# One core: pairs of edge tiles with one addition a pair in the first attention layer, and part of its weighing on VectorE

## What is computed

```python
score = jnp.einsum('ehc,ehc->eh', q[dst], k[src]) / np.sqrt(C)   # H = 4 heads of C = 64
m = jax.ops.segment_max(score, dst, num_segments=N)
ex = jnp.exp(score - m[dst])
denom = jax.ops.segment_sum(ex, dst, num_segments=N)
alpha = ex / denom[dst]
msg = alpha[:, :, None] * v[src]
agg = jax.ops.segment_sum(msg, dst, num_segments=N)
out = agg.reshape(N, H * C) + h @ Wskip + bskip
return x + jax.nn.relu(out)
```

## Time and profile before

| | |
|---|---|
| median of 3 runs | 8399.73 us (8396.39 to 8405.45) |
| the profiled execution, its own time | 8395.49 us |
| its span | 8393.8 us |
| busy over the whole span: PE, DVE, ACT, POOL | 70%, 63%, 37%, 62% |
| first layer's loop, start of its first and its last score product | 681.8 and 1947.0 us |
| DVE, PE, ACT, POOL busy in 900 to 1100 us | 172.94, 159.41, 169.91, 134.34 of 200.00 us |
| granted TensorE clock, DMA share there | 0.96, 0.61 |

### The profile page before, as it was taken

One profiled execution on the slowest core, in us unless ns is written; L12 is line 12 of the kernel. 1 busy time (PEld: TensorE's weight loads), 2 busy tenths in 40 slices (PEclk: granted clock), 3 DMA queues, 4 the chain that ended last, 5 costly groups with the idle time before them and its releaser, 6 DMA issues. The chain is left out here.

```text
span 8393.8 us, 114926 instructions
## 1 busy us (share of the span) xinstructions
PE 5911.5 (70%) x29083; PEld 4485.9 (53%) x29083; DVE 5252.3 (63%) x14320; ACT 3102.5 (37%) x9138; POOL 5186.5 (62%) x5153
## 2 busy tenths in 40 slices
PE   6586777774399555556688888965577775574398
PEld 5234555553387234444577777754455553453387
DVE  9867888887665576665544444446677777435544
ACT  1245888887422300000333333312344444312322
POOL 0475666665577677777677777756777771433422
PEclk9798999996599877778699999967789986686599
DMA  5475666563366333333111111116333343473366
GB/s 147 152 247 160 171 173 172 170 172 115 108 207 200 111 102 101 100 102 103 28 28 32 31 28 32 26 27 193 102 105 103 105 100 117 150 229 95 100 204 199
DMA packets 633946, 1017.21 MB, mean 121 GB/s; under 512 B 136434, under 2 KB 436482, under 8 KB 631948
## 3 DMA queue, kind: packets, MB, share of 16 engines
q0 software_dynamic: 241920, 540.19, 24.2%
q1 hardware_dynamic: 391436, 470.18, 17.7%
HBM read 790.98 MB, written 222.86 MB: 121 GB/s over the span
## 5 line engine op out<-in xcount | busy, mean ns | idle before, releaser
L4099 POOL DMA_INDIRECT gat_edges_rows<-gat_table,gat_room x1080 | 1115.5, 1033 | 340.9 <-issue 322.4
L2825 POOL DMA_INDIRECT l_edges_ring<-pairs,first_room x832 | 843.8, 1014 | 472.5 <-issue 242.2
L2387 POOL DMA_INDIRECT l_sum_rows<-l_feats,back_room x832 | 827.0, 994 | 265.7 <-issue 241.9
L2407 PE MATMUL l_sum_o<-l_sum_rows,l_sum_s 128*128 128x256 f32 x1664 | 604.4, 523 | 468.3 <-DVE l_sum_s L2418 220.4
L2876 ACT ACTIVATE l_edges_ring<-l_edges_ring,l_edges_weight 128x64 f32<-128x64 f32 x3328 | 816.4, 335 | 0.0
L2407 PEld LDWEIGHTS l_sum_o<-l_sum_rows,l_sum_s 128*128 128x128 f32 x1664 | 410.9, 261 | 655.0 <-DVE l_sum_s L2418 325.5
L2948 PE MATMUL l_edges_o<-l_edges_ring,l_edges_sf 128*128 128x260 f32 x1664 | 534.9, 427 | 149.8 <-DVE l_acc L3081 141.1
L3717 ACT ACTIVATE m_ffn_ht<-m_ffn_hp,m_ffn_b1t 128x256 f32<-128x256 f32 (+1 forms) x598 | 270.7, 453 | 815.5 <-PE m_ffn_hp L3684 810.3
L2429 DVE TENSOR_TENSOR l_acc<-l_acc,l_sum_o 128x256 f32 x832 | 350.1, 421 | 351.3 <-PE l_sum_o L2407 258.4
L3694 PE MATMUL m_ffn_yp<-m_ffn_w2b,m_ffn_ht 128*128 128x256 f32 x2156 | 502.1, 385 | 30.4 <-ACT m_ffn_ht L3717 29.8
L3684 PE MATMUL m_ffn_hp<-m_ffn_xt,m_ffn_w1b 128*128 128x256 f32 (+1 forms) x2392 | 509.0, 366 | 11.5 <-DVE m_ffn_xt L3733 7.2
(11 more groups left out here) (899 smaller groups left out, 14604.4 us busy)
## 6 DMA issues: line engine op xcount, KB each, us to landing
sorted_rows<-l_proj_zero SPq DMA_DIRECT2D x44, 1032.0 KB
m_ffn_w1b<-in_L_ffn_w SPq DMA_DIRECT2D x32, 1024.0 KB, 6.4
m_ffn_w2b<-in_L_ffn_w SPq DMA_DIRECT2D x32, 1024.0 KB, 5.4
m_ffn_xs<-sorted_rows SPq DMA_DIRECT2D x120, 258.0 KB, 3.6
m_ffn_w1b<-in_L_ffn_W SPq DMA_DIRECT2D x57, 512.0 KB, 4.6
m_ffn_w2b<-in_L_ffn_W SPq DMA_DIRECT2D x57, 512.0 KB
m_by_node<-gat_edges_ys SPq DMA_DIRECT2D x96, 256.0 KB
l_proj_taken<-m_by_node SPq DMA_DIRECT2D x28, 768.0 KB, 6.9
```

The costliest lines, as they stand in the source:

```text
L2387: pool.indirect_dma_start(rows[:, slot, j, :], None, table, bass.IndirectOffsetOnAxis(ap=L.src[:, t:t + 1], axis=0)).then_inc(got[slot], 16)
L2407: pe.matmul(o[:, j, 0:D], s4[:, q % S4, j, :], rows[:, slot, j, :], start=True, stop=True).then_inc(out_done, 1)
L2825: pool.indirect_dma_start(rows(q, 0, 2 * D)[:, j, :], None, table, bass.IndirectOffsetOnAxis(ap=L.src[:, t:t + 1], axis=0)).then_inc(got[q ...
L4099: pool.indirect_dma_start(rows[:, slot, j, :], None, table, bass.IndirectOffsetOnAxis(ap=L.src[:, q * B + j:q * B + j + 1], axis=0)).then_ ...
```

## The change

The list is now cut into pairs of columns (`group=2`): both tiles of a pair belong to one block. That gives 391 pairs and 49 more visits of pairs, 440 pairs or 880 tiles, 220 quads, 55 chunks (`SortedList.tiles`). The two matmuls of a pair add up in one PSUM bank (`start` on the first, `stop` on the second), and VectorE adds once a pair. In odd quads ScalarE weighs three tiles (12 multiplications) and VectorE the fourth in one instruction (`weigh_last`), in step q+10 right behind `onehot`; a semaphore, `eighth`, tells PE and ACT. The ring of selection matrices has 13 places in place of 14. The sorter gets a factor `group` in its numbers; the other lists keep `group=1`.

```diff
-        self.tiles = -(-(self.cols + T) // (2 * Q)) * 2 * Q
+        self.tiles = -(-(-(-self.cols // group) + T) * group // (2 * Q)) * 2 * Q
...
-    H, W, n, CQ, U, BK = 4, D, L.quads, 4, 14, 2
+    H, W, n, CQ, U, BK, G = 4, D, L.quads, 4, 13, 2, L.group
...
                         act.wait_ge(lowered, c + 1)
+                        if c >= 2:
+                            act.wait_ge(eighth, (c - 1) * CQ // 2)
...
-                    for j in range(Q):
+                    for j in range(Q - q % 2):
                         for h in range(H):
                             v = rows(q, h * (W // H), (h + 1) * (W // H))[:, j, :]
                             act.activation(v, v, ACT.Identity, scale=p[:, h, t0 + j:t0 + j + 1])
...
                     pe.wait_ge(weighed, q + 1)
+                    if q % 2:
+                        pe.wait_ge(eighth, q // 2 + 1)
                     for j in range(Q):
-                        t = q * Q + j
-                        if t >= BK:
-                            pe.wait_ge(acc_own, t - BK + 1)
-                        pe.matmul(o[:, t % BK, 0:W + H], sf[:, q % 2, j, :], rows(q, 0, W + H)[:, j, :], start=True, stop=True
-                                  ).then_inc(out_done, 1)
+                        k, i = divmod(q * Q + j, G)
+                        if i == 0 and k >= BK:
+                            pe.wait_ge(acc_own, k - BK + 1)
+                        pe.matmul(o[:, k % BK, 0:W + H], sf[:, q % 2, j, :], rows(q, 0, W + H)[:, j, :], start=(i == 0),
+                                  stop=(i == G - 1)).then_inc(out_done, 1)
...
-                    for j in range(Q):
-                        t = q * Q + j
-                        dve.wait_ge(out_done, t + 1)
-                        if t:
-                            dve.wait_ge(acc_own, t)
+                    for j in range(0, Q, G):
+                        k = (q * Q + j) // G
+                        dve.wait_ge(out_done, (k + 1) * G)
+                        if k:
+                            dve.wait_ge(acc_own, k)
                         a = acc[:, ds(b[j], 1), :]
-                        dve.tensor_tensor(a, a, o[:, t % BK, 0:W + H].unsqueeze(1), ALU.add).then_inc(acc_own, 1)
+                        dve.tensor_tensor(a, a, o[:, k % BK, 0:W + H].unsqueeze(1), ALU.add).then_inc(acc_own, 1)
                         yield
...
+                def weigh_last(q, slot):
+                    if q % 2 == 0:
+                        return
+                    c, t = q // CQ, q % CQ * Q + Q - 1
+                    dve.wait_ge(weight_ready, c + 1)
+                    v = rows(q, 0, W)[:, Q - 1, :].rearrange("p (h k) -> p h k", h=H)
+                    dve.tensor_tensor(v, v, weight[:, c % 2, :, t:t + 1].to_broadcast([P, H, W // H]), ALU.mult
+                                      ).then_inc(eighth, 1)
...
-        first, back = SortedList(nc, "first", E), SortedList(nc, "back", E)
+        first, back = SortedList(nc, "first", E, group=2), SortedList(nc, "back", E)
```

More of the change, by code:

```diff
@@ L662, with __init__ @@
 class SortedList:
-    def __init__(self, nc, name, edges):
-        self.name, self.edges = name, edges
+    def __init__(self, nc, name, edges, group=1):
+        self.name, self.edges, self.group = name, edges, group
         self.cols = -(-edges // P)
-        self.tiles = -(-(self.cols + T) // (2 * Q)) * 2 * Q
+        self.tiles = -(-(-(-self.cols // group) + T) * group // (2 * Q)) * 2 * Q
         self.quads = self.tiles // Q
@@ L694, with __init__ @@
 class SortConstants:
-    def __init__(self, nc, ctx, core, tiles, when):
+    def __init__(self, nc, ctx, core, tiles, when, group=1):
         sb = lambda n, s, dt=F32: ctx.enter_context(nc.sbuf_tensor(f"sort_{n}_{when}", s, dt))
@@ L720, in _ @@
                     dve.tensor_copy(self.slot[:], slot_i[:])
-                    dve.tensor_scalar(self.tile_of[:], tile_i[:], -1.0, None, ALU.add)
+                    dve.tensor_scalar(self.tile_of[:], tile_i[:], -float(group), None, ALU.add)
                     for k in range(8):
@@ L899, in vector @@
         settled()
-        did(dve.tensor_reduce(self.ended[:], self.cmp, AX.X, ALU.add))
+        did(dve.tensor_reduce(self.ended[:], self.cmp[:, :, L.group - 1::L.group], AX.X, ALU.add))
         yield
@@ L909, in vector @@
         dve.wait_ge(self.summed, 1)
-        did(dve.tensor_tensor(self.first[:], self.banks[0:T, 0, 0:1], core.part[0:T, :], ALU.add))
+        did(dve.tensor_scalar(self.first[:], self.banks[0:T, 0, 0:1], core.part[0:T, :], float(L.group), ALU.add, ALU.mult))
         settled()
@@ L918, in vector @@
             dve.wait_ge(self.counted, c + 1)
-            did(dve.tensor_tensor(self.tile, const.slot[:, at], n, ALU.subtract))
+            did(dve.scalar_tensor_tensor(out=self.tile, in0=n, scalar=-float(L.group), in1=const.slot[:, at],
+                                         op0=ALU.mult, op1=ALU.add))
             did(dve.tensor_scalar(L.block[0:1, at], n[0:1, :], -1.0, None, ALU.add))
@@ L2766, in edge_attend @@
     AWAY = (LANE_SLOTS - 1) * LANE_SETS
-    assert n % CQ == 0
+    assert n % CQ == 0 and Q % G == 0 and L.tiles // 2 <= 512
     with Phase(nc, name) as ph:
@@ L2806, in edge_attend @@
              "acc_own", "faded")]
-        copied, lasts, linked = ph.sem("copied"), ph.sem("lasts"), ph.sem("linked")
+        copied, lasts, linked, eighth = ph.sem("copied"), ph.sem("lasts"), ph.sem("linked"), ph.sem("eighth")
         got = [ph.gathered_sem(k) for k in range(LANE_SETS)]
@@ L3066, in add @@
                         if q:
-                            dve.wait_ge(acc_own, q * Q)
+                            dve.wait_ge(acc_own, q * Q // G)
                         a = acc[:, ds(b[0], 1), :]
@@ L3074, in add @@
                         dve.wait_ge(faded, 2 * (q // CQ + 1))
-                    for j in range(Q):
-                        t = q * Q + j
-                        dve.wait_ge(out_done, t + 1)
-                        if t:
-                            dve.wait_ge(acc_own, t)
+                    for j in range(0, Q, G):
[3 more added lines that the diff above has]
+                            dve.wait_ge(acc_own, k)
                         a = acc[:, ds(b[j], 1), :]
-                        dve.tensor_tensor(a, a, o[:, t % BK, 0:W + H].unsqueeze(1), ALU.add).then_inc(acc_own, 1)
+                        dve.tensor_tensor(a, a, o[:, k % BK, 0:W + H].unsqueeze(1), ALU.add).then_inc(acc_own, 1)
                         yield
-                steps(dve, n, [(4, score), (12, add), (0, onehot), (5, within), (6, across), (7, under)], **whole)
+                def weigh_last(q, slot):
[6 more added lines that the diff above has]
+                                      ).then_inc(eighth, 1)
+                steps(dve, n, [(4, score), (12, add), (0, onehot), (5, within), (6, across), (7, under), (10, weigh_last)],
+                      **whole)
 class Core:
@@ L3185, in layer0_gnn @@
     with ExitStack() as cs:
-        const = SortConstants(nc, cs, core, first.tiles, "a")
+        const = SortConstants(nc, cs, core, first.tiles, "a", first.group)
         project(nc, core, "l0_proj", core.x, 4 * D,
```

## The result

| | before | after |
|---|---|---|
| median of five runs | 8403.12 us (8396.39 to 8413.97) | 8449.41 us (8444.88 to 8457.54) |
| the profiled execution, its own time | 8395.49 us | 8457.54 us |
| first layer's loop, first to last score product | 1265.2 us | 1319.4 us |

The ratio is 1.0056, 95% interval 1.0046 to 1.0067: the changed kernel is 46 us slower. The loop alone is 54.2 us longer. The two profiled executions lie 62 us apart; the 8 us that the loop doesn't explain are of the size of the spread of the runs, and the profiled one of the changed kernel is the slowest of its five.

A forecast was written before the change was run, and what follows sets the result against it. It took the first layer's loop for a ring of waits, no full engine: 54.75 chunks x 23.52 = 1287.7, plus 37 is 1324.7, less 1265.2 is +59.5. On 8395.5 that gives 8455 us, range 8400 to 8510.

The forecast's parts named there:

- The sum: First layer's loop: 54.75 chunks x 23.52 plus 37 us gives 1324.7, +59.5 us; the kernel 8455 us.
- Step 1: From `far` through exponentials and multiplications to S3's first collect: 6.42 us, nothing in this chain changes.
- Step 2: S3's to S0's first collect: 5.46 us where it was 6.92, ScalarE deciding once PE's 2.00 wait goes; gain 1.46.
- Step 3: S0's to S1's first collect: matmuls, last addition, then two dependent scans, 6.34 us where it was 5.89; loss 0.45.
- step 4: S1's first collect to the next `far`: matmuls 3.90, addition 0.34, two dependent scans; 5.30 us.
- ring of engines: PE's matmuls wait for VectorE's step, VectorE's last addition for PE's last matmul: 23.52 us a chunk against 23.67.
- The ring of the gathers: Score sum's end, GpSimd's gather, landing, next product: 22.3 to 23.3 us a chunk, below 23.52 in all cases.
- The rival that the gathers decide: First layer's loop: engines keep out of the way, chunk 22.3 to 23.3 us, +20 us, 8416; chance 0.19.
- The kept 37 us: Of the loop's 40 us of GpSimd pauses and smaller lateness, 37 stay, as 880 gathers still hold seven pauses.
- slower still: Rival: lateness passed on whole, by port lock or slow PE stages; chunk 24.2 to 24.4, 8495 to 8505; chance 0.22.
- The rule on the port pair: The multiplication behind `onehot` would stretch gather issues, up to 0.34 us twice a chunk; loop some 26 us longer.
- Shorter instructions: Rival rule that merging VectorE instructions lengthens others' waits; said to show in steps 3 and 4, no chance of its own.

The follow-up runs named there:

- late order: Changed kernel with the second addition of a quad two turns later, behind the scans again: 8415.9 us, ratio 1.0007.
- PSUM edit: Score product written over the query in PSUM, not over the key: kernel before 8327.49 us, late order 8320.56 (repeat 8325.04), changed kernel 8436.92.
- the second pair: Kernel before with the PSUM edit, without and with `weigh_last`, one addition a tile: 8327.49 and 8370.63 us, loops 1182.9 and 1221.7.
- the fastest: Changed kernel with the late order and the PSUM edit together: 8320.56 us, ratio 0.9908; run again 8325.04 us, 0.9896.

## Why the prediction was right, point by point

**The sum.** Forecast 8455, measured 8449.41; the loop +59.5 forecast, +54.2 measured.

**Step 1**, 6.42, measured 6.37. **Step 2**, 5.46, measured 5.35: `collect` waits for no addition, and ScalarE decides. Its size is confirmed from the other side, by the run of pairs with ScalarE weighing all (24.24 less 23.28 is 0.96, as worked out). **Step 3**, 6.34, measured 6.31, and **step 4**, 5.30, measured 5.25: the last addition behind PE and two scans behind that. The late order shows it is these scans: with the addition behind them steps 3 and 4 take 5.44 and 4.23, and the loop is 36 us shorter. The estimate of 0.06 between dependent scans is 0.04 in the trace (1318.09 + 0.41 to 1318.54).

**"The halved additions take 0.15 us out of a chunk and no more."** This comparison was wrong, though the sum wasn't. The 23.67 of before was not the pace of its ring of engines. That is 22.55, as the PSUM edit on it shows, and as eight chunks of its own trace do. The score products that wait for landings in the earlier trace rows and the 2.00 us at PE in the earlier trace rows (0.72 with the gathers out of the way) held it up by the rest. What failed is the reading of the chunk at 1281.66 as undisturbed: it was not, the gathers already held it up before the change. At its own pace the changed kernel's ring of the engines is 0.73 longer, not 0.15 shorter.

Put together from 22.55, the +54.2 is three more chunks (3 x 22.55 = 68), the longer ring (54.75 x 0.73 = 40) and 53 less of everything that comes on top of the ring (98.2 before, which is 1265.2 less 51.75 x 22.55; 44.8 after). The forecast had +71, -8 and -3. So as an account of what the change does two terms were far off and cancelled, and that is luck. The absolute length of the loop after was not: it was built up step by step and each step came out. Step 4 had no value of before beside it; it was 4.33 (the `far` of 1303.63 less 1299.30), and the loss of 0.92 there is twice that of step 3.

**The ring of the gathers**, 22.3 to 23.3 and below the engines' 23.52: that it stays below is right, by the PSUM edit, which leaves 23.28 alone. The rival that the gathers decide falls with it. Its size is less certain. In the late order, where landings do hold VectorE up, the chunks at the full clock take 22.3 us in the mean, but nine chunks take only 21.5 to 21.9, under the lower end.

**The kept 37 us.** The loop less 54.75 x 23.28 (1274.6) is 44.8. The size held, its content didn't. I had taken what came on top in the kernel before for seven pauses of GpSimd and smaller lateness, and gave the clock no part in it. But its 25 chunks with a stretch at half the clock take 25.9 us in the mean and the others 23.1. In the changed kernel the 15 chunks of 24.9 give 25 us over 23.28, the five that hold a pause 19 us (1.7 to 5.4 each, and four of them hold a stretch at half the clock as well), and the first chunk 3 (together 47, less some 2 at the loop's ends). The rival "slower still" had one PE stage in three some 2 us longer as something that the change would add (its own terms give 8492 to 8503 us, a little under the 8495 to 8505 stated). That lateness is there, in 15 of 54 chunks at 1.7 us, but it was there before the change too, and it did not grow. The forecast was near because the undisturbed chunk came out 0.24 shorter (13 us) and this remainder 8 larger.

**The rule on the port pair.** The issue at 1313.14, beside `onehot` and the multiplication, takes 1.65 us where the next takes 0.95:

```profile
1313.14 1.65 POOL L2826 DMA_INDIRECT l_edges_ring<-pairs,first_room  x1 [0.30 <-issue]
1315.09 0.95 POOL L2826 DMA_INDIRECT l_edges_ring<-pairs,first_room  x1 [0.30 <-issue]
```

Before, such an issue took 1.42. Of the changed kernel's 880 issues 116 take over 1.15 us, and 112 of these overlap a `onehot`; most often they take 1.33 or 1.34. All that the issues take above 0.95 us adds up to 60 us, where it was 53 for 832 issues before, so the multiplication lengthened them little. It cost nothing in the changed kernel, whose ring is the engines'. What it costs where the gathers decide is not shown, since the late order has few such issues. The Trainium skill (SBUF — State Buffer, Who interferes with whom) says that a VectorE instruction with two SBUF inputs contends with a GpSimd instruction that reads SBUF, and not with one that only writes it. The prediction left that condition out, and no run here shows which of the two a gather issue is. The longer issue agrees with such a contention; the 26 us worked out from it did not come.

**Shorter instructions.** The loss of steps 3 and 4 is not that an addition was merged but where the merged one stands: the late order has the same instructions. The Trainium skill (Perfetto Trace Analysis, Optimizing Scalar/DVE Operations) advises to break instructions up where an engine that isn't saturated holds others up. The runs agree and show a cheaper remedy: with ScalarE weighing all, the additions taken apart again (the longer list alone) bring the loop from 1376.5 to 1341.7, and the merged ones in the late order to 1328.3.

**What stays open.** Why PE's clock falls in some S1 steps of the changed kernel and not in others was not settled: PE waited 0.56 and 0.98 us before the collects at half the clock shown above and 0.57 and 0.98 one chunk later, where the clock stayed. Between kernels the stretches are more where PE waits longer (with ScalarE weighing all) and fewer with the PSUM edit in two orders of three. No run took the pauses of GpSimd themselves away.

## What to carry to other kernels

Where engines run interleaved in a fixed order, ask of each instruction that gets merged or dropped what now stands behind the handoff from the other engine; independent work belongs in front of the wait, and here two turns in the order were worth 36 us of loop. Where two rings are close, measure each at its own pace by opening the other, before crediting an edit with the difference of two chunks. A long chunk next to shorter ones of the same kernel is not undisturbed: compare with the shortest that repeat, and look at the granted clock in the longer chunks before and after. The same relief can gain or lose by what is on the ring: one multiplication moved between engines took 57 us out of the loop behind the pairing and put 39 in without it (both kernels of the second pair with the PSUM edit).

## What the runs showed of the hardware

- The product written to PSUM takes as long as to SBUF, 1.22 us for 128x1024 fp32, and the sum read from it 1.21 us.
- The cost of a fallen clock comes in steps: one stretch at half the clock puts 1.5 to 1.7 us into a chunk whose steps are otherwise the same, before the change (step 4 5.9 against 4.3) as after it (6.9 against 5.25). The mean granted clock from 750 to 1850 us hides it: 0.96 in the kernel before, 0.97 in the changed one and 0.99 in the fastest.
- With the gate opened earlier, GpSimd issued its gathers back to back for whole chunks at 21.4 us each (861 of 880 in the late order follow the one before by 0.35 us or less). Most take 0.95 us, one in most chunks 1.84. Its pauses of some 3 us stayed, as in

```profile
1133.53 0.94 POOL L2826 DMA_INDIRECT l_edges_ring<-pairs,first_room  x1 [3.09 <-issue]
```
